# A convolution, attention and expert kernel: a late sum in the second pair, a projection in banks of its own, TensorE's loop begun behind the attention, halves normed in turn

## What is computed

```python
# 1: attention over channels (c = 32), then a residual
attn = softmax(einsum('bcn,bnd->bcd', queries, keys)); x = conv1x1(attn @ values, Wo, bo) * gamma + x
# 2: on the layer-normed tokens t (1024 x 256), 8 heads of 32
a1 = softmax(q1 @ k1.T / 32**0.5); a2 = softmax(q2 @ k2.T / 32**0.5)
o = (a1 - lam * a2) @ v                    # then a group norm over (64 channels x 1024 tokens)
t = t + group_norm(o) @ out_w.T + out_b
# 3: on the layer-normed tokens: a shared expert and 8 routed ones, of which each token takes two
t = t + shared(x) + sum_e combine[:, e] * (silu(x @ W_gate[e]) * (x @ W_up[e])) @ W_down[e]
```

## Time and profile before

| | |
|---|---|
| median of 3 runs | 6316.64 us (6312.25 to 6323.77) |
| profiled execution: its time | 6318.59 us |
| its span (first to last instruction) | 6316.6 us |
| mean granted TensorE clock | 0.977 of full speed |
| TensorE busy | 5874.0 us, 93% |
| VectorE, ScalarE, GpSimd busy | 75%, 51%, 49% |
| chain that ended last | PE 74%, DVE 10%, issue 7% |

### The profile page before, as it was taken

One profiled execution on the slowest core, in us unless ns is written; L12 is line 12 of the kernel. 1 busy time (PEld: TensorE's weight loads), 2 busy tenths in 40 slices (PEclk: granted clock), 3 DMA queues, 4 the chain that ended last, 5 costly groups with the idle time before them and its releaser, 6 DMA issues.

```text
span 6316.6 us, 127368 instructions
## 1 busy us (share of the span) xinstructions
PE 5874.0 (93%) x41264; PEld 3812.3 (60%) x41264; DVE 4745.7 (75%) x6583; ACT 3225.0 (51%) x5788; POOL 3094.2 (49%) x1382
## 2 busy tenths in 40 slices
PE   6999999999998999989999999999999999999998
PEld 3565565655656556565565656656566565665656
DVE  5867778687786877868778687776877768777786
ACT  3545545455454544635456354554545545455454
POOL 2716537175370743807447073471735717256271
PEclk8999999999999999999999999999999999999999
DMA  2212222122222222222122221222212222121221
GB/s 73 56 47 57 57 52 51 56 53 56 48 51 59 50 56 53 46 59 55 54 50 46 58 57 56 51 49 56 56 52 52 48 61 56 46 57 44 64 56 44
DMA packets 148339, 339.07 MB, mean 54 GB/s; under 512 B 38224, under 2 KB 60880, under 8 KB 139216
## 3 DMA queue, kind: packets, MB, share of 16 engines
q1 hardware_dynamic: 147664, 330.38, 21.5%
HBM read 90.49 MB, written 17.30 MB: 17 GB/s over the span
## 4 chain that ended last, share of the span: by engine, by line
PE 74%; DVE 10%; issue 7%; ACT 3%; DMA 2%; POOL 2%; SPq 0%; DVEq 0%; ACTq 0%; POOLq 0%
PE psum L1033 17%; PE psum L1257 15%; PE psum L1182 13%; PE psum L1203 11%; DVE minus_max L767 7%; PE psum L1324 6%; PE psum L1210 5%; PE psum L1284 2%; POOL prob_sums L377 2%; PE psum L1188 1%; PE psum L1082 1%; DMA prob_sums<-combine_rows_dram 1%; DMA stack<-stage 1%; DVE small L682 1%; ACT stage L473 1%
## 5 line engine op out<-in xcount | busy, mean ns | idle before, releaser
L377 POOL TENSOR_TENSOR prob_sums<-probs 128x1024 f32<-128x1024 f32 x752 | 1794.6, 2387 | 3053.6 <-ACT probs L522 2713.1
L522 ACT ACTIVATE probs<-psum 128x512 f32<-128x512 f32 x4096 | 2218.1, 596 | 1496.8 <-PE psum L1257 1484.4
L767 DVE TENSOR_REDUCE minus_max<-psum 128x1 f32<-128x1024 f32 x2048 | 2421.6, 1219 | 341.1 <-PE psum L1182 311.0
L1257 PE MATMUL psum<-stack 98*128 98x512 f32 x4096 | 1429.6, 434 | 2.4 <-DVE max_rows L777 2.0
L377 POOL TENSOR_TENSOR prob_sums<-prob_sums,probs 128x1024 f32<-128x1024 f32 x512 | 1218.1, 2379 | 44.5 <-ACT probs L522 6.8
L1182 PE MATMUL psum<-stack 96*128 96x512 f32 x4096 | 1206.4, 408 | 29.3 <-DMA stack<-stage 12.9
L1203 PE MATMUL psum<-probs,v_tokens 128*32 128x256 f32 x16384 | 1118.5, 388 | 0.0
L1257 PEld LDWEIGHTS psum<-stack 98*128 98x128 f32 x4096 | 701.3, 190 | 545.6 <-ACT probs L522 336.9
L1182 PEld LDWEIGHTS psum<-stack 96*128 96x128 f32 x4096 | 763.9, 193 | 259.9 <-DVE max_rows L777 44.6
L1033 PE MATMUL psum<-act_hi,w_hi 128*128 128x512 f32 x1730 | 693.7, 401 | 67.7 <-issue 29.2
L1203 PEld LDWEIGHTS psum<-probs,v_tokens 128*32 128x32 f32 x16384 | 422.4, 109 | 473.5 <-issue 272.1
(11 more groups left out here) (152 smaller groups left out, 4687.6 us busy)
## 6 DMA issues: line engine op xcount, KB each, us to landing
stack<-stage SPq DMA_DIRECT2D x1024, 128.0 KB, 3.1
stack<-stage SPq DMA_DIRECT2D x256, 256.0 KB, 3.0
prob_sums<-combine_rows_dram SPq DMA_DIRECT2D x128, 256.0 KB, 3.9
stage<-combine_rows_dram SPq DMA_DIRECT2D x128, 256.0 KB, 4.1
x_tile<-x_dram SPq DMA_DIRECT2D x17, 1024.0 KB, 4.8
x_tile<-o_head SPq DMA_DIRECT2D x512, 32.0 KB, 1.9
stack<-max_rows SPq DMA_DIRECT2D x512, 4.0 KB
y_dram<-residual SPq DMA_DIRECT2D x16, 512.0 KB, 4.2
```

What stands on the lines that cost most here:

```text
L377: nc.gpsimd.tensor_tensor(total, first, probs[:, k % NP, :], ALU.add).then_inc(sum_pool, 1)
L522: nc.scalar.activation(probs[:, k % NP, half * HALF:(half + 1) * HALF], ps[:, exp_bank(k) + half, :], ACT.Exp).then_inc(p_ready, 1)
L767: v.tensor_reduce(nm[:, u % 2, q:q + 1], flat_in, AX.X, ALU.max, negate=True).then_inc(ring_free, 1)
L1257: mm(ps[:, exp_bank(k) + half, :], stack[0:KS, s, 1, kt * P:(kt + 1) * P], stack[0:KS, s, 0, half * HALF:(half + 1) * HALF], start=True, s ...
```

## The change

Five things are changed. (1) The ones-matmuls of group 2 go behind the second pair of the next unit, and both reciprocals into its third pair (tiles 4 and 5). (2) proj 3 leaves the ring: its twelve matmuls follow proj 2 at once, into banks 4 and 5, VectorE takes its low halves around the first maximum, and the values stand one tile behind each of the first six scores and two tiles behind the turn, in banks 6, 7, 4, 5. (3) TensorE's code is cut in two functions, and its loop now holds "behind the attention of b, then attention of b + 1", with the first attention in front of the loop and the last rest behind it. The other engines' loops stay as they are. (4) The low part of head group 0's second half goes ahead of VectorE's wait for the last head, and two of the last head's four copies are issued by ScalarE. (5) In the layer norm ScalarE takes tiles 0, 1, 4, 5 and VectorE 2, 3, 6, 7, and TensorE waits for each half apart.

```diff
-    late = {2: ((u, 0),), 0: ((u - 1, 1), (u - 1, 2))}.get(pair, ())
+    late = {2: ((u, 0),), 0: ((u - 1, 1),), 1: ((u - 1, 2),)}.get(pair, ())
...
-    before = [("proj", 0), ("proj", 1), ("proj", 2), ("score", 0, 0), ("score", 0, 1), ("part", 3, 0, 0), ("score", 0, 2),
-              ("part", 3, 1, 0)]
-    before += [("score", 0, q) for q in range(3, NT)] + [("turn", 0)]
+    before = [("proj", 0), ("proj", 1), ("proj", 2), ("score", 0, 0)]
+    before += [("score", 0, q) for q in range(1, NT)] + [("turn", 0)]
...
+VALUES_BEHIND = {("score", 0, q): (q,) for q in range(6)}
+VALUES_BEHIND["turn", 0] = (6, 7)
+VALUE_BANK = (6, 7, 4, 5)
...
-RECIP_AT, HEAD_AT = (2, 5), 7
+RECIP_AT, HEAD_AT = (4, 5), 7
...
# SyncE, load_stack
-                        sp.wait_ge(ring_free, b * len(RING) + last[2 * m + 1] + 1)
+                        if m == 0:
+                            sp.wait_ge(ring_free, b * len(RING) + RING_AT["proj", 1] + 1)
+                        else:
+                            sp.wait_ge(k2_low, b * NH + NH)
...
-                    for c in range(4):
+                    for c in range(4 if h < HEADS - 1 else 2):
...
# ScalarE, normalise
-                for k in range(2):
+                for k in (0, 2):
...
# ScalarE, head of the attention
-                copy_values(0)
-                copy_values(1)
                 act.wait_ge(y_out[1], b * 16 + 16)
                 for half in range(NH):
-                    project_part(3, half, 0)
-                copy_values(2)
-                copy_values(3)
+                    act.wait_ge(k2_full, b * NH + half + 1)
+                    take_projection(3, half, 0, ps[:, 4 + half, :])
+                for k in range(4):
+                    copy_values(k)
...
# ScalarE, behind the normed halves of head group 0
+                act.wait_ge(oh_ready, (b + 1) * HEADS)
+                for c in (2, 3):
+                    h = HEADS - 1
+                    nc.scalar.dma_start(ocm[HD * (h % 4):HD * (h % 4) + HD, h // 4, c * CQ:(c + 1) * CQ],
+                                        oh[HD * c:HD * c + HD, h % 2, :]).then_inc(o_in[h % 2], 16)
...
# VectorE, normalise
-                for k in range(2, 4):
+                for k in (1, 3):
...
# VectorE, head of the attention
+                def k2_low_part(half):
+                    dve.wait_ge(proj_hi, b * PROJ_STEPS + 6 + half + 1)
+                    v.scalar_tensor_tensor(stage[:, 1, 3, cols].bitcast(F32R), ps[:, 4 + half, :], vec(V_K2B),
+                                           stage[:, 0, 3, cols], ALU.add, ALU.subtract).then_inc(k2_low, 1)
                 for item in BEFORE:
                     ring_step(item)
+                    if item == ("proj", 2):
+                        k2_low_part(0)
+                    if item == ("score", 0, 0):
+                        k2_low_part(1)
...
+                norm_low(0, 1)
                 for s in range(2):
                     dve.wait_ge(o_in[s], (b + 1) * (HEADS // 2) * 4 * 16)
...
-                    if half == 0:
-                        norm_low(0, 1)
...
# TensorE
+                    if tt in (4, 6):
+                        pe.wait_ge(k2_low, b * NH + tt // 2 - 1)
...
                 for item in BEFORE:
                     ring_step(item)
+                    if item == ("proj", 2):
+                        for half in range(NH):
+                            split_mm(ps[:, 4 + half, :], W_QK + 3 * CT * C, (C, P),
+                                     slice(half * HALF, (half + 1) * HALF)).then_inc(k2_full, 1)
...
-                    pe.wait_ge(n_act, b * 2 + 2)
-                    pe.wait_ge(n_dve, b * 2 + 2)
                     for k in range(4):
+                        if k % 2 == 0:
+                            pe.wait_ge(n_act, b * 2 + k // 2 + 1)
+                            pe.wait_ge(n_dve, b * 2 + k // 2 + 1)
...
+            attention(0)
+            with pe.Fori(0, B - 1) as b:
+                behind_attention(b)
+                attention(b + 1)
+            behind_attention(B - 1)
```

More of the change, by code:

```diff
@@ L273, in load_stack @@
                     if u < 2:
-                        last = [RING_AT["proj", t] if ("proj", t) in RING_AT else RING_AT["part", t, 1, 0] for t in range(4)]
                         sp.wait_ge(proj_hi, b * PROJ_STEPS + 4 * m + 2)
                         sp.dma_start(*q_parts[1]).then_inc(stack_in[s], 16)
-                        sp.wait_ge(ring_free, b * len(RING) + last[2 * m] + 1)
+                        sp.wait_ge(ring_free, b * len(RING) + RING_AT["proj", 2 * m] + 1)
                         sp.dma_start(*q_parts[0]).then_inc(stack_in[s], 16)
@@ L1139, in tokens, with norm_groups, attention @@
                         last.then_inc(t_full, 1)
[L1141 to L1155 removed]
+            def norm_groups(b, t):
+                pe.wait_ge(g_stat, b * CT + t + 1)
+                mm(ps[:, 4 * t, 0:4], wf[:, F_BLK:F_BLK + P], small[:, 88 + 4 * t:92 + 4 * t],
+                   start=True, stop=True).then_inc(g_full, 1)
+            def attention(b):
                 def ring_step(item):
```

45 lines of the change are left out of this document (20 added, 25 removed).

## The result

The changed kernel takes 6149.4 us (median of four runs, 6143.7 to 6155.7), beside 6317.4 for the kernel before (now also four runs, 6312.3 to 6323.8): a ratio of 0.9734, 95% interval 0.9717 to 0.9751, 168 us faster. Forecast were 6140 and 177 us. The profiled execution took 6151.4, 167.2 less than that of before.

What follows compares the result with a forecast made beforehand. TensorE, busy 93% of the span, was taken as the bound. Terms of 5.9, 4.2 and 1.1 make 11.2 us a batch, 179 over sixteen, less 2: 177 off 6318.6, about 6140 us; range 6090 to 6205.

Steps and rivals of the forecast that it cites:

- Late sum: Steady attention: moving one ones-matmul group into the 0.48 us hole before the turn gains 0.42 in fourteen units, 5.9 a batch.
- the reciprocal would cost nothing: Steady attention: VectorE's first reciprocal, 0.95 us, moves from second to third pair; nothing was charged for it.
- GpSimd would be served in the old place: Steady attention: the sums group GpSimd waits on is still taken where it was before; nothing charged.
- Head: Start of the attention: gains of 2.2 and 3.1 less 0.9 make 4.4 us a batch, taken as 4.2 for the clock.
- (a): Ahead of the first score: moving TensorE's branch removes a 1.65 us gap; the first score comes 2.2 earlier.
- (b): First score to turn, 14.2 us before: fewer waits and one low part make it 3.4 shorter, taken as 3.1.
- (c): Turn to first exponential's matmul: two value tiles behind the turn lengthen it from 4.3 to about 5.2 us, costing 0.9.
- Behind the attention: After the attention, up to the transposes: an earlier low part and halves normed in turn gain 1.1 us a batch.
- The branch: TensorE's loop branch, moved behind the last ones-matmuls: its 1.65 us gap would fall in an existing wait of 2.07.
- the halves normed in turn: Layer norm: the first half is complete after two ScalarE tiles, so the transposes start about 0.7 us sooner.
- the slower one (VectorE as the bound): Steady units: the moved reciprocal delays a release by 0.95, making the kernel 34 us slower, 6351; chance 0.05.
- The rival of a clock that stays up: Head and behind the attention: shorter idle times keep TensorE's clock up, saving 3 us more a batch, 6092; chance 0.10.

Runs made afterwards that it cites:

- the run with both sums late: Changed kernel with the first pair's other group of ones-matmuls moved into the second pair too: 6696.1 us, 1.0583 of the kernel before.
- putting the branch back: Changed kernel with TensorE's loop as before, its branch ahead of the attention: 6182.0 us, 0.9772 of the kernel before.
- own banks alone: Kernel before with only the fourth projection in its own banks, its low parts ahead of the maxima and the values placed as changed: 6291.9 us, ratio 0.9952.
- the run with the values ahead of the turn: Changed kernel, still one batch per loop body, last two value tiles behind the head's seventh and eighth score: 6130.1 us, 0.9695 of the kernel before.
- the kernels without a loop: Changed kernel, last values ahead of the turn, all batches written out on TensorE (6125.4 us, 0.9685), or on TensorE and VectorE (6121.0 us, 0.9682).
- the loop of five: Changed kernel, last values ahead of the turn, five batches in TensorE's loop body: 6108.2 us, 0.9661 of the kernel before.

## Why the prediction was right, and where not

The forecast (6140, 6090 to 6205) was 9 us from the result. Two of its three terms hold one by one; the third comes out half a microsecond short a batch, from two errors that partly cancel, and within the head a larger gain and a larger loss than reckoned cancel as well. That the total lies so near is in part luck.

- **Late sum, 5.9 a batch.** Measured 6.10 (212.27 to 206.17), and 97 us by undoing it. That the reciprocal would cost nothing holds; that GpSimd would be served in the old place was the condition it all hung on, as the run with both sums late shows.
- **Head, 4.2.** Measured 2.27 + 3.59 - 1.38 - 0.56 = 3.92. (a) The 2.2 ahead of the first score was right. The prediction shows no working for what exceeds 1.65, and that is the branch's too: putting the branch back costs all of it and more (2.49), own banks alone win 0.09 there. The gap itself is 1.64 in the mean of the kernel before (1.74 with the branch back); the earlier trace rows has shorter issue waits beside it (of its 26, eleven are 0.2 to 0.8 us, nearly all some 3 us behind the branch, 0.3 a batch in all), and these went too. That leaves 0.3 of the 2.27 open; with the branch back, where 0.5 is left, the lower clock of that run is enough for it. (b) 3.59 against 3.1. (c) 1.38 against 0.9, and 0.56 against the 0.2 set aside for the clock. But 0.56 is hardly more than a difference of two such means scatters (0.4), and the clock doesn't carry it: in the changed kernel 7.2 us between the first exponential and the second turn are at the lower level, in the one before 6.4, while between turn and exponential it is the other way round (1.2 and 2.2). What holds the two stretches up together, 1.94, is in the main where the last values stand: the run with the values ahead of the turn has 1.69 less.
- **Behind the attention, 1.1.** Measured 0.64, from two errors that partly cancel. The edits are worth 1.89 where the branch is elsewhere (41.41 to 39.52) and 2.26 beside it, not 1.35: the halves normed in turn give some 1.3 to 1.4 where 0.7 was reckoned, by the stretch from the next convolution's values to the transposes (5.28 before, 3.94 in the changed kernel, 3.87 with the branch back). **The branch is the step that failed:** it was charged 0.3, at most 0.9, and costs 1.08 at the first high part and 1.25 up to the transposes. The reasoning that the gap is hidden in a wait of 2.07 took 1.65 as the branch's price. Behind the attention batches 0 and 15, with no branch there, show 2.06, the others 2.98 to 3.38.
- **What is late next**: the transposes wait 0.39 rather than 0.7, and the values of the next convolution now wait for the load of x (0.15 to 1.35 in most batches).

Sum: 6.10 + 3.92 + 0.64 = 10.66 a batch against 11.2. The two rules of the Trainium skill (Advanced Engine Details and Errata, Control Flow Timing; Runtime: NRT & Kernel Launch, Instruction fetch mechanics) can now be weighed: with 51 or 108 ns, moving the branch or halving the number of branches would show nothing; the runs show 1.1 to 2.5 us for each. The second names such a stall, without a figure, and agrees. It adds that kernels prefer full unrolling where possible: here the kernels without a loop (0.9685 and 0.9682) can't be told from the loop of one (0.9695), and are 13 to 17 us behind the loop of five (0.9661).

Of the rivals, the slower one (VectorE as the bound) never came near: the scores' waits for maxima rose by 1 us a batch, all at the head of the attention, none in the unit shown. The kernel could be made slower by such a move, but through GpSimd, and with the other group. The rival of a clock that stays up didn't come either: 15.9 us of a batch are at the lower level in both kernels.

## What to carry to other kernels

A hole in front of a waiting instruction can be filled with work taken from a stretch without waits, if no one queues behind the moved work: ask first which buffer it frees. A branch back in a loop isn't free because it stands in a wait that is longer than the gap it leaves elsewhere: here it cost 1.0 to 1.1 us in either of two waits of 1.4 to 2.1 us. With a few batches in the body most of it goes. Work put behind a step that others wait for belongs in front of it if the engine idles there.

## What the runs showed of the hardware

TensorE's branch leaves a longer idle time where the matmuls ahead of it have themselves been waited for. TensorE idles for 1.4 to 2.0 us behind it where a run of matmuls without waits stands ahead of it (15 branches each in the kernel before and in the one with the branch back), and for 3.0 to 3.6 us at the first high part behind the attention, where 2.06 to 2.08 are there without a branch. From the start of the last ones-matmuls to the first one behind the branch these are 3.6 to 4.2 us, and 2.7 without a branch (3.66 in the rows 1096.38 and 1100.04 of the changed kernel). Between the two low parts it is 3.1 to 4.1 (3.60 in the rows 1101.95 and 1105.55).

A unit of the attention takes 14.01 us where TensorE's batches are written out and VectorE's stand in a loop, and 13.91 to 13.92 where both are in a loop, of one, two or five batches on TensorE. It shows in the same kernel too: the changed kernel's batch 0, ahead of TensorE's loop, needs 207.31 for its fourteen units, its batch 15, in the loop, 206.06. With both engines' batches written out it is 13.91 in all sixteen, so code that is written out is not slower in itself. Nor is it the amount fetched. TensorE's instruction queue (the one whose packets change when its loop does), in the changed kernel and in both without its loop (packets, MB, share):

```profile
q8 instruction: 379, 6.21, 0.4%
```

```profile
q8 instruction: 326, 5.34, 0.4%
```

What costs the 0.09 when TensorE's batches alone are written out was not tried and stays open.
